# Two halves of ZP added by TensorE's ones product instead of by POOL, in a two-layer cross-attention kernel

## The reference

```python
q = heads(hidden_states @ W_q)
probs_t = softmax(einsum('bhsd,bhtd->bhst', q, k_t) * attn_scale)
text_out = einsum('bhst,bhtd->bhsd', probs_t, v_t)
qsem = _l2norm(einsum('bhst,bte->bhse', probs_t, text_ehs))
sem = einsum('bhse,bne->bhsn', qsem, _l2norm(ip_ehs))
fused = einsum('bhsd,bhnd->bhsn', q, k_ip) * attn_scale + SEM_SCALE * sem
ip_out = einsum('bhsn,bhnd->bhsd', softmax(fused) * mask, v_ip)
```

## Time and profile before

| what | value |
|---|---|
| median of 3 runs | 1776.63 us (1776.45 to 1779.87) |
| the profiled execution | 1777.33 us |
| its span, first to last instruction | 1775.2 us |
| PE matmul busy | 1640.1 us (92%) |
| DVE busy | 1431.6 us (81%) |
| ACT busy | 1039.1 us (59%) |
| POOL busy | 819.4 us (46%) |
| mean granted TensorE clock | 0.976 of full speed |

### The profile page before, as it was taken

How to read it: one execution, slowest core, us unless ns; L and a number is a source line. 1 busy time by engine, 2 the same in 40 slices (tenths; PEclk the granted TensorE clock), 3 DMA queues, 4 the chain that set the end, 5 groups by cost and what they waited for, 6 DMA issues and landing times.

```text
span 1775.2 us, 42550 instructions
## 1 busy us (share of the span) xinstructions
PE 1640.1 (92%) x14568; PEld 1449.5 (82%) x14568; DVE 1431.6 (81%) x3639; ACT 1039.1 (59%) x2204; POOL 819.4 (46%) x682
## 2 busy tenths in 40 slices
PE   4999999999999999817999999999999999999986
PEld 4888888888888888617888888888888888888865
DVE  4677777777777778643999899999999999999884
ACT  3466666666666666513666666666666666666652
POOL 4222222222222222153576566656666566656563
PEclk9999999999999999958999999999999999999998
DMA  6344444444444443143323322342233322332211
GB/s 172 102 115 119 119 117 122 119 120 118 120 119 119 119 119 92 55 135 106 91 77 94 97 63 78 102 103 75 65 95 104 93 66 83 102 90 66 66 28 38
DMA packets 186210, 172.35 MB, mean 97 GB/s; under 512 B 25854, under 2 KB 185998, under 8 KB 185998
## 3 DMA queue, kind: packets, MB, share of 16 engines
q1 hardware_dynamic: 185998, 169.64, 34.4%
HBM read 109.86 MB, written 57.59 MB: 94 GB/s over the span
## 4 chain that ended last, share of the span: by engine, by line
PE 44%; DVE 6%; POOL 2%; issue 2%; SPq 1%; ACT 1%; DMA 1%; DVEq 0%; POOLq 0%; ACTq 0%
PE MISC L61 13%; PE GP L61 12%; PE PV L785 4%; PE NAT L734 4%; PE TR L755 3%; DVE ZP L1102 3%; PE PV L788 2%; PE MISC L825 1%; DVE PM L1108 1%; PE MISC L826 1%; PE MISC L878 1%; PE PV L745 1%; PE MISC L805 1%; POOL ZS L1212 1%; POOL RN L1252 1%
## 5 line engine op out<-in xcount | busy, mean ns | idle before, releaser
L1212 POOL TENSOR_TENSOR ZS<-ZP 128x256 f32<-128x256 f32 x320 | 315.2, 987 | 308.7 <-DVE ZP L1102 306.8
L315 ACT ACTIVATE P<-TA 128x512 f32<-128x512 f32 x320 | 202.0, 632 | 251.8 <-DVE TA L462 251.3
L1108 DVE SCALAR_TENSOR_TENSOR PM<-P,PH 128x512 f32<-128x512 f32 x320 | 299.0, 934 | 0.0
L61 PE MATMUL GP<-PH,GH 128*128 128x256 f32 (+1 forms) x960 | 250.9, 291 | 38.3 <-DVE ZP L1102 36.3
L1102 DVE TENSOR_TENSOR ZP<-GP,PM 128x512 f32<-128x512 f32 x320 | 218.8, 684 | 36.4 <-PE GP L61 30.9
L61 PE MATMUL GP<-PH,GL 128*128 128x256 f32 (+1 forms) x960 | 243.1, 282 | 0.0
L447 DVE TENSOR_REDUCE MX<-NAT 128x2 f32<-128x154 f32 x320 | 101.8, 318 | 167.7 <-PE NAT L143 166.1
L1094 DVE TENSOR_REDUCE MX<-NAT 128x2 f32<-128x504 f32 x320 | 213.7, 669 | 16.5 <-PE NAT L734 15.9
L61 PEld LDWEIGHTS GP<-PH,GH 128*128 128x128 f32 (+1 forms) x960 | 181.1, 189 | 54.8 <-ACT PH L931 30.0
L462 DVE TENSOR_TENSOR TA<-TR,ST 128x512 f32<-128x512 f32 x320 | 219.1, 686 | 3.0 <-PE TR L163 2.8
L931 ACT CAST PH<-P 128x512 fp32r<-128x512 f32 x320 | 198.8, 621 | 28.7 <-ACT P L927 0.7
(11 more groups left out here) (226 smaller groups left out, 4299.8 us busy)
## 6 DMA issues: line engine op xcount, KB each, us to landing
QS<-qk_parts SPq DMA_DIRECT2D x480, 64.0 KB, 2.7
qk_parts<-PARTS SPq DMA_DIRECT2D x96, 224.0 KB, 2.7
CT<-in_ctx_t SPq DMA_DIRECT2D x32, 512.0 KB, 4.4
KS<-qk_parts SPq DMA_DIRECT2D x240, 64.0 KB, 2.7
KS<-qk_parts SPq DMA_DIRECT2D x240, 63.0 KB, 2.9
qk_parts<-PARTS SPq DMA_DIRECT2D x48, 192.0 KB, 2.3
QS<-NH SPq DMA_DIRECT2D x480, 4.0 KB
qk_parts<-PARTS SPq DMA_DIRECT2D x32, 220.5 KB, 3.5
```

What stands on the lines that cost most here:

```text
L61: ins = e.matmul(out, lhs, rhs, start=(n == 0), stop=(n == len(pairs) - 1))
L315: e.activation(P[:, s % NP, :], TA[:, s % 2, :], ACT.Exp, scale=SCALE).then_inc(q["exp"], 1)
L1108: e.scalar_tensor_tensor(PM[:, s % 2, :], P[:, s % NP, :], 2.0, PH[:, s % NS, :].bitcast(F32), ALU.mult, ALU.subtract).then_inc(q["pm"], 1)
L1212: e.tensor_tensor(ZS[:, s % NZ, :], ZP[:, s % 2, 0:S], ZP[:, s % 2, S:2 * S], ALU.add).then_inc(q["zs"], 1)
```

## The change

POOL's addition of the two halves of ZP (L1212) is left out, and with it the tile ZS and the semaphore `zs`. ZP gets `NZ` = 6 buffers of 512 columns in place of 2. PV's product with E21 is made for each half of ZP, 8 products a group in place of 4. DVE's ZP now waits for `pv` before it takes up a buffer again, and once for `once` (the product that reads the weights staged in ZP). PE waits for `zp` in place of `zs`. ONES becomes a view of the first tile of FU.

```diff
-    ZP, ZS = sb("ZP", [128, 2, 2 * S]), sb("ZS", [128, NZ, S])
+    ZP = sb("ZP", [128, NZ, 2 * S])
-    E21, ONES, HALF = sb("E21", [128, SLOT]), sb("ONES", [128, 128]), sb("HALF", [128, NIP])
+    E21, HALF = sb("E21", [128, SLOT]), sb("HALF", [128, NIP])
...
-    vi_raw = stage(ZS[:, :, :].rearrange("p r n -> p (r n)"), 0, KC)
+    vi_raw = stage(ZP[:, :, :].rearrange("p r n -> p (r n)"), 0, KC)
...
+    ONES = FU[:, 0, :, :].rearrange("p a n -> p (a n)")[:, 0:128]
...
-                e.wait_ge(q["zs"], HG * g + HG)
+                e.wait_ge(q["zp"], HG * g + HG)
...
-                for j, h, r in heads:
-                    ins = e.matmul(PV[SLOT * j:SLOT * (j + 1), 0:S], E21[:, :], ZS[:, (HG * g + j) % NZ, :], start=False, stop=True)
+                for i in range(2):
+                    for j, h, r in heads:
+                        ins = e.matmul(PV[SLOT * j:SLOT * (j + 1), 0:S], E21[:, :], ZP[:, (HG * g + j) % NZ, i * S:(i + 1) * S],
+                                       start=False, stop=i == 1)
...
-                if s >= 2:
-                    e.wait_ge(q["zs"], s - 1)
+                if s >= NZ:
+                    e.wait_ge(q["pv"], (s - NZ) // HG + 1)
                 e.wait_ge(q["pm"], s + 1)
                 e.wait_ge(q["gp"], s + 1)
-                e.tensor_tensor(ZP[:, s % 2, :], GP[:, :], PM[:, s % 2, :], ALU.mult).then_inc(q["zp"], 1)
+                if s == 0:
+                    e.wait_ge(q["once"], 2)
+                e.tensor_tensor(ZP[:, s % NZ, :], GP[:, :], PM[:, s % 2, :], ALU.mult).then_inc(q["zp"], 1)
...
-            s = t - 2
-            if 0 <= s < B * H:
-                if s == 0:
-                    e.wait_ge(q["once"], 2)
-                if s >= NZ:
-                    e.wait_ge(q["pv"], (s - NZ) // HG + 1)
-                e.wait_ge(q["zp"], s + 1)
-                e.tensor_tensor(ZS[:, s % NZ, :], ZP[:, s % 2, 0:S], ZP[:, s % 2, S:2 * S], ALU.add).then_inc(q["zs"], 1)
```

More of the change, by code:

```diff
@@ L700, in layer1 @@
                    "stack4 mrow0 mrow1 store fill clear clear_q w_hi w_lo xt_hi xt_lo ct_hi ct_lo qk qk_f qk_hi qk_lo gr vc gh gl w_cip w_ip once once_s once_q norm rn ctn "
-                   "vall_out vip_in kbd scm sc vip vm v nat mx mxt nh nm tr exp ph pm gp zp zs pv pvs ont on cmb nrm fu fexp tx "
+                   "vall_out vip_in kbd scm sc vip vm v nat mx mxt nh nm tr exp ph pm gp zp pv pvs ont on cmb nrm fu fexp tx "
                    "ptt pt hst ht_hi ht_lo om y")
@@ L896, in _ @@
                 e.wait_ge(q["fill"], FILLS)
-                product(e, k[:, 0:NIP], [(ONES[:, :], SQ[:, c, :]) for c in range(KC)]).then_inc(q["norm"], 1)
+                product(e, k[:, 0:NIP], [(ONES, SQ[:, c, :]) for c in range(KC)]).then_inc(q["norm"], 1)
     @block.scalar
@@ L1047, in _ @@
         e.memset(E21[:, :], 0.0).then_inc(q["fill"], 1)
-        e.memset(ONES[:, :], 1.0).then_inc(q["fill"], 1)
+        e.memset(ONES, 1.0).then_inc(q["fill"], 1)
         e.memset(HALF[:, :], 0.5).then_inc(q["fill"], 1)
```

## The result

| | before | after |
|---|---|---|
| median, first comparison | 1777.91 us (1776.45 to 1779.87) | 1793.90 us (1789.92 to 1797.98) |
| ratio | | 1.0089 [1.0063, 1.0116] |
| profiled execution | 1777.33 us | 1789.92 us |
| its span | 1775.2 us | 1787.8 us |
| one batch, from NAT to NAT | 58.04 us | 58.98 us |

The first comparison has four runs of each kernel, and 1776.63 us is the median of the first three before.

A forecast was written before the change was run, and what follows sets the result against it. PE was taken to bound the kernel, with short stands waiting for DVE's ZP. 1777.33 + 34.9 - 1.4 - 10.6 = 1800.2, less 0.7 for the median, gave 1799.5 us, with 1787 to 1812 as the range.

The forecast's parts named there:

- The bound: Second layer: PE, busy 56.08 of 58.04 us a batch, sets the pace; added PE work costs nearly its full price.
- Term 1: PE's added products in PV: +34.9 us, 0.43 for each of 79 groups and 0.89 for the last.
- Term 2: POOL's 320 additions gone: 0 of itself, -1.4 us together from PV's few waits; waits passed to DVE are free.
- Term 3: DVE's PM no longer held up by POOL's additions, so PE waits less for ZP: -10.6 us.
- place A: 13 steps where an addition following XTSL holds up PM, so ZP comes late: 13 x 0.48 = 6.2 us back.
- place B: 14 steps where CTSL holds up PM: 0.49 each stays, 4.1 of 11.0 us comes back under the longer PV.
- place C: 15 waits of about 0.5 us, round trip between PE and DVE through bank GP: stays, but for 0.3 us.
- Sum of term 3: Total relief from PM's hold-ups: 6.2 at place A, 4.1 at place B, 0.3 in two early batches; bounds 0 and 36.3.
- Rival 2: DVE's lag causes all PE's stands, so with PM at 0.68 PE never stands: 1773.1 us; chance 0.10.
- Rival 1: No relief comes back; DVE stays late at place A and place B, PM held up elsewhere: 1810 us; chance 0.17.
- Rival 3: PV's new products hide in time PE would have waited anyway, at half price: 1782 us; chance 0.05.
- Rival 4: Second order cost, lower clock for busier PE or ACT late with P: some 5 us more, 1805; chance 0.08.

The follow-up runs named there:

- E21: Not a run: the weights tile in the code for PV's product over ZP; the change makes that product for each half of ZP.
- experiment 3: Kernel before with 4 more products a group over ZS, a tile of zeros as weights, all POOL additions kept: 1799.22 us, ratio 1.0101.
- experiment 4: Kernel before with POOL adding the halves of all heads in place in the sixfold ZP, ones tile placed as in the change: 1776.93 us, ratio 1.0004.
- experiment 6: Kernel before with POOL's additions for heads 9 and 10 of each batch made memsets: 1769.71 us in one run, a batch of 57.53 us.
- experiment 2: Changed kernel with PV's norm product over the left half of ZP alone, right half left out of the norm: 1757.75 us, ratio 0.9871.
- experiment 7: Kernel before with POOL's addition for head 11 of each batch made a memset: 1782.07 us in one run, a batch of 57.85 us.
- second comparison: Changed kernel run again unaltered beside the kernel before: 1794.25 us against 1781.96 us, ratio 1.0069.

## Why the prediction was right, and what it missed

- **The bound.** Right. PE's order sets the pace, and what is added to it is paid, in all five places of a batch (experiment 3).
- **Term 1, 34.9 us.** The price of 0.43 a group was exact: 0.86 for the two halves in the chain, and experiment 3 paid it five times a batch. One part of it was wrong, the last group. Its 0.89 us came from a stretch at half clock: from 1745.33 to 1748.15 us the granted clock was 0.50. Over the last PV of the changed kernel, from 1758.80 to 1760.77 us, it was 1.00; PE had stood for 1.62 us before the one and for 0.76 us before the other. The two chains have, before and after:

```profile
1745.33 1.93 PE PV L785 x16
1747.26 0.89 PE PV L788 x8
```

```profile
1758.80 1.07 PE PV L786 x16
1759.87 0.90 PE PV L790 x16
```

  So the last group got cheaper by 0.85 us with twice the E21 work.
- **Term 2, POOL.** Right in size: the last PV waits those 0.76 us for ZP where it waited 1.62 for ZS, and experiment 4 shows that the waits passed to DVE are free. That nobody but PV waited for the additions is wrong. In the last batch DVE's ZP waited for POOL to free one of its two buffers:

```profile
DVE ZP L1102 <- POOL ZS L1212: 3.2, 5, 0.6
```

  These waits were worth nothing to PE. Experiment 4 makes the additions but has no such wait, and PE waits for ZP 36.4 us in it, where it was 36.3.
- **Term 3, place A.** The size was right, 0.49 a batch. The cause it named holds (experiment 6). That the relief comes from taking the additions away was luck in part: experiment 3 keeps them and has the same relief from PE's longer PV. And where the prediction says that POOL had begun two additions by 1323.31, it had begun one.
- **Term 3, place B.** The size was right, the ground half: B goes to 0.49 under a longer PV, as forecast (experiment 3), and also without one once no addition follows CTSL and holds FU up (experiment 2).
- **Term 3, place C.** Right, unchanged in every kernel.
- **The step that was mis-sized** is "Sum of term 3: 6.2 + 4.1 + 0.3 = 10.6". It left out the step behind A, 0.43 us a batch. I had looked for hold-ups in PM alone and for stands of PE only where a row had a bracket. In that step PE stood without one:

```profile
1328.73 0.48 PE L734 MATMUL NAT<-KS,QS 65*128 65x256 f32 x2
...
1329.49 0.36 PE L61 MATMUL GP<-PH,GH 128*128 128x256 f32 x1
...
1330.53 1.07 PE L785 MATMUL PV<-P,VB 128*32 128x256 f32 x16
```

  GP began 0.76 us after NAT, and PV 1.04 us after GP, where the changed kernel has 0.55 and 0.81: 0.44 us together. What DVE had lost there was NRM's 0.5 us behind the addition of head 11, and experiment 7 gets 0.43 back by making that one addition a memset. The view that would have shown it is DVE's groups: NRM at 732 ns for 40 columns beside the 0.25 that the chain shows for it in the tail.
- **The sum.** The forecast was 10.3 us too high on the profiled executions. The 12 batch lengths that follow the first batch's second softmax (its transposes, L813, at 948 us in both) grew by 10.6 us (697.3 to 707.9) where the forecast has 12 x 1.44 = 17.3: 6.7 us, of which 12 x 0.43 = 5.2 are the step behind A. The length before the last softmax went from 47.03 to 46.59 where I had 1.7 more: 2.15 us, mostly the half clock. And the layer's first GP came 1.2 us earlier (836.7, where it was 837.9), which has nothing to do with the change: the last NAT of the first layer, which is the same in both kernels, is earlier by 1.4 us already. That is 10.1; the rest I did not follow.
- **Rivals.** Rival 2 (DVE's lag is the root of all stands) fell: experiment 2 has all of DVE's relief and PE still waits 25.4 us for ZP. Rival 1, which has DVE as late as before at A and B, fell with the relief there. Rival 3 is refuted as put: the products don't hide, the step behind A was relieved by as much as they cost. Rival 4 did not show: the granted clock was 0.977 in the profiled execution, where it was 0.976, and no step grew by more than the product's price.

What stays open: the medians of the first comparison differ by 16.0 us and the profiled executions by 12.6; in the second comparison it is 12.3. The full batches of the changed kernel's two profiles agree within 0.03 us, so nothing speaks for another order of the work. Only one run of the kernel before was profiled, and no run shows where the 3 us between the comparisons lie.

## What to carry to other kernels

When two engines hold each other up over SBUF, read the mean of every small instruction against its own shortest time, not that of the costliest alone: a 0.23 us product held up for 0.5 us was worth 0.43 us a batch, half of all that the forecast had for DVE's relief. A hold-up can go for nothing by ordering the two engines with a wait, which here beat both the kernel with the collision and the kernel that bought its absence on PE. And a step that does not grow under a price is no proof that the price is free there: only the two halves of the change, run apart (experiments 2 and 3), showed that it was paid in all five places and that in one of them a relief of the same size stood against it.

## What the runs showed of the hardware that I had not expected

PM can stand for more than one POOL instruction. At place A two additions of some 0.7 us each run from 1323.28 to 1324.70; PM is issued at 1323.40, during the first, and ends 0.56 us behind the second. The prediction has whoever comes later blocked, and there the second addition, which came later, went first. It is not always so. In experiment 3 PM is issued at 1272.78, during the first of the same two additions, and takes 0.74 us, while the two additions take 1.88 us in place of 1.42: PM went between them. At place B of the kernel before, PM ends 0.54 us behind CTSL, and it is the addition next in POOL's order that is longer, 1.19 us, and then FU behind it (the first two lines in experiment 2). So a waiting DVE instruction can be passed by the next POOL instruction or go ahead of it, and no run shows what decides.

The same program is granted a different clock in different executions. The first layer is untouched by every experiment, and yet in its stretch from 65 to 90 us the column of the granted clock has 0.93 in ten of the thirteen profiles and 0.66 in three. The kernel before, and then experiment 4:

```profile
65.00:90.00 25.00, 22.32 (x190) 17.71 (x189) 17.76 (x74) 14.43 (x33) 3.49 (x4) 0.93 0.37 110
```

```profile
65.00:90.00 25.00, 23.65 (x143) 18.68 (x143) 13.49 (x57) 10.90 (x25) 2.18 (x3) 0.66 0.30 91
```

In experiment 4 the granted clock is 0.50 from 72 to 80 us, in the kernel before it is 0.97 there. As means of full and half clock, 0.93 is 3.5 us at half clock and 0.66 is 17, which would cost some 7 us more (an estimate from the two rows). In those three profiles the second layer's first GP comes at 841 to 845 us, in the others at 835 to 839, while the batch of experiment 4 is that of the kernel before (57.99 and 58.04). That is why the experiments are judged here by the length of a batch first and by the median second. What the engine did just before does not tell them apart: from 60 to 65 us PE is busy for 3.83 us in experiment 4 and for 5.00 in the kernel before, but for 3.84 in experiment 2, which is one of the ten.
